# Cross attention and the heads in one block, with the first two tiles of the heads loaded in cross attention's last turn

## The reference

```python
x = x + cross_attention(layernorm(x), ctx, ...)   # 16 heads of 64: softmax(q k^T) v, then @ w_out + b_out, times tanh(gate)
x = x + attention_over_heads(layernorm(x), W_Q, W_K, W_V)   # per token, 16 heads of 32: softmax(Q) (softmax(K)^T V)
x = x + mlp(layernorm(x), w_gate, w_up, w_down)   # silu(x wg) * (x wu), then wd; int weights times 1/127
```

## Time and profile before

| | us |
|---|---|
| three runs | 1935.17, 1937.47, 1942.68 (median 1937.47) |
| the profiled execution | 1935.26 |
| its span, first to last instruction | 1933.5 |

### The profile page before, as it was taken

The page is one execution under the profiler, slowest core; times in us unless marked ns, Lnnn a source line. Parts: engine busy times, 40 slices in busy tenths (PEclk is TensorE's granted clock), DMA queues, the critical chain, the costliest instruction groups (busy, mean ns, idle before and its releaser), DMA issues. The chain is left out here.

```text
span 1933.5 us, 36622 instructions
## 1 busy us (share of the span) xinstructions
PE 1869.3 (97%) x14096; PEld 1611.8 (83%) x14096; DVE 1039.6 (54%) x2015; ACT 667.4 (35%) x1356; POOL 558.1 (29%) x546
## 2 busy tenths in 40 slices
PE   6989999999999999999999999599999999999999
PEld 4868888988988898898889889488888788888887
DVE  6614555455455545545554554478889863333322
ACT  3234444444444444444444444231111231111111
POOL 3015335433533543453354345331112000000000
PEclk9989999999999999999999999799999999999999
DMA  7323313322331332233132224623333041001000
GB/s 242 129 80 93 89 54 109 93 70 76 99 97 54 109 88 75 76 98 98 55 109 86 73 80 131 181 78 99 98 114 111 31 150 42 24 23 43 13 31 22
DMA packets 166629, 165.65 MB, mean 86 GB/s; under 512 B 8688, under 2 KB 123888, under 8 KB 166576
## 3 DMA queue, kind: packets, MB, share of 16 engines
q1 hardware_dynamic: 162144, 156.27, 26.7%
q10 hardware_dynamic: 4432, 8.65, 1.2%
HBM read 131.08 MB, written 33.82 MB: 85 GB/s over the span
## 5 line engine op out<-in xcount | busy, mean ns | idle before, releaser
L497 POOL TENSOR_TENSOR x_prob<-x_prob,x_share 128x256 f32<-128x256 f32 x256 | 157.0, 613 | 621.6 <-DVE x_share L664 614.3
L82 PE MATMUL x_ps<-w_cT_hi,w_space_hi 128*128 128x258 f32 x1024 | 299.2, 292 | 5.8 <-DVE w_space_lo L688 5.8
L83 PE MATMUL x_ps<-w_cT_lo,w_space_hi 128*128 128x258 f32 x1024 | 290.2, 283 | 0.0
L84 PE MATMUL x_ps<-w_cT_hi,w_space_lo 128*128 128x258 f32 x1024 | 288.9, 282 | 0.0
L681 DVE COPY x_mix<-x_ps 128x512 f32<-128x512 f32 x256 | 176.1, 688 | 115.2 <-PE x_ps L84 115.1
L688 DVE TENSOR_TENSOR w_space_lo<-x_ps,w_space_hi 128x512 fp32r<-128x512 f32 x256 | 162.5, 682 | 99.6 <-ACT w_space_hi L789 67.2
L82 PE MATMUL x_ps<-x_pT_hi,x_cn_hi 128*128 128x512 f32 x512 | 208.1, 406 | 1.5 <-DVE x_mix L681 1.5
L778 ACT ACTIVATE x_prob<-x_ps,x_negmax 128x257 f32<-128x257 f32 x256 | 121.9, 476 | 240.1 <-DVE x_negmax L659 240.1
L82 PEld LDWEIGHTS x_ps<-w_cT_hi,w_space_hi 128*128 128x128 f32 x1024 | 193.9, 189 | 12.7 <-DVE w_space_lo L688 8.9
L84 PE MATMUL x_ps<-x_pT_hi,x_cn_lo 128*128 128x512 f32 x512 | 201.3, 393 | 0.0
L83 PE MATMUL x_ps<-x_pT_lo,x_cn_hi 128*128 128x512 f32 x512 | 199.7, 390 | 0.0
(11 more groups left out here) (205 smaller groups left out, 3550.1 us busy)
## 6 DMA issues: line engine op xcount, KB each, us to landing
e_raw_T<-ctx_T SPq DMA_DIRECT2D x64, 514.0 KB, 4.0
e_raw_n<-ctx_nat SPq DMA_DIRECT2D x64, 512.0 KB, 3.6
q<-q_q ACTq DMA_DIRECT2D x16, 512.0 KB, 2.8
e_q<-q SPq DMA_DIRECT2D x16, 512.0 KB, 4.1
o_hi<-x_o_hi SPq DMA_DIRECT2D x32, 256.0 KB, 2.6
o_lo<-x_o_lo SPq DMA_DIRECT2D x32, 256.0 KB, 3.1
a_oT_hi<-o_hi SPq DMA_DIRECT2D x16, 512.0 KB, 4.3
a_oT_lo<-o_lo SPq DMA_DIRECT2D x16, 512.0 KB, 5.6
```

The lines of the kernel that those rows point to most:

```text
L82: pe.matmul(out, lhs[0], rhs[0], start=start, stop=False)
L83: pe.matmul(out, lhs[0], rhs[1], start=False, stop=False)
L84: return pe.matmul(out, lhs[1], rhs[0], start=False, stop=stop)
L497: pool.tensor_tensor(prob[:, i, 0:KT * P], prob[:, i, 0:KT * P], share[:, i:i + 1].to_broadcast([P, KT * P]), ALU.mult)\
```

## The change

Cross attention and heads_and_mlp each return their engine programs, and `build` runs both in a single block: no barrier between them. identity (`ident`) and the PSUM tensor are allocated once for both. The tensors of the heads lie in SBUF from the place where those of cross attention begin (`start`), ordered so that what is filled early lies over what cross attention has finished with; those of cross attention move by the size of `ident`.

Parts of the heads' start move into cross attention's last turn. On SP `first_loads(0)` (tile 0) goes in front of the weight pieces 12 to 15, and `first_loads(1)` (tile 1, then mask, bias and gate) behind them, ahead of the first store. On ACT tanh comes ahead of the second output copy; on DVE the bias product comes behind the second output split; on POOL the bias is added to tiles 0 and 1 ahead of the splits of pieces 16 and 18. DVE's splits of pieces 17 and 19 move behind the scaling of tile 0 (`late_weights`). PE begins with a wait for w_out's splits, does the out-projections of tile 0 (bank Y) and tile 1 (bank DOTS) one after the other, then the transposes of tile 0; it has new waits for the later splits ahead of keys and values. SP's first MLP weight piece waits for all 20 splits, tile 2's load for all stores of cross attention, and MLP piece 22 for the store of tile 14. The diff, without changes of indentation and cut to its core:

```diff
-def cross_attention(nc, hw, ahead, ...):
-    with ExitStack() as ctx:
+def cross_attention(nc, ctx, ps, ident, hw, ahead, ...):
-        ident = s.sb("ident", [P, P])
-        ps = s.psum()
-        block = ctx.enter_context(nc.Block())
-        @block.sync
-        def _(sp):
+    def sync(sp, first_loads):
...
-                    load_w(range(PAIRS + 2, RING + 4))
+                load_w(range(PAIRS + 2, RING))
+                first_loads(0)
+                load_w(range(RING, RING + 4))
+                first_loads(1)
                 store_out(t, 0)
...
-            sp.wait_ge(o_stored.sem, 32 + TURNS * o_stored.per)
...
-                    w_low(pool, range(0, PIECES, 2))
+                w_low(pool, range(0, 16, 2))
+                first_bias()
+                w_low(pool, range(16, PIECES, 2))
...
                 low_out(t, 1)
                 if not more:
-                    w_low(dve, range(15, PIECES, 2))
+                first_bias()
+                w_low(dve, (15,))
...
                     w_high(range(RING, 16))
+                first_tanh()
                 high_out(t, 1)
...
+    def late_weights(dve):
+        w_low(dve, range(17, PIECES, 2))
...
-        area = Area(nc, "a", nc.sbuf_base)
+    area = Area(nc, "a", start)
...
+    def first_loads(sp, part):
+        c, last = cross, cross.last
+        if part == 0:
+            sp.wait_ge(c.mixed.sem, c.mixed.at(last, 3 * c.mixed.per // c.batches))
+            sp.wait_ge(c.turned.sem, c.turned.at(last, c.turned.per))
+            sp.wait_ge(c.last_ready.sem, c.last_ready.at(last, c.batches))
+        sp.wait_ge(c.o_stored.sem, c.o_stored.at(part + 1, 0))
+        load(sp, 0, part)
+        if part == 1:
+            sp.wait_ge(c.mixed.sem, c.mixed.at(last, c.mixed.per))
+            for dst, src in ((mask[:, :], same_token), (gated_bias[:, :], bias.partition_broadcast(P)),
+                             (gate_b[:, :], gate.partition_broadcast(P))):
+                sp.dma_start(dst, src).then_inc(once, 16)
...
                     sp.wait_ge(y_ready.sem, y_ready.at(t, i + 1))
                     sp.wait_ge(x1_done.sem, x1_done.at(t, i + 1))
-                    load(t, i + 2)
+                if tile_of(t, i) == 0:
+                    sp.wait_ge(cross.o_stored.sem, cross.o_stored.at(cross.last + 1, 0))
+                load(sp, t, i + 2)
...
             def load_w(numbers):
                 for n in numbers:
+                if n == 0:
+                    for done in cross.w_lo_done:
+                        sp.wait_ge(done, len(hw.pieces) // 2)
...
-            for dst, src in ((ident[:, :], identity), (mask[:, :], same_token),
-                             (gated_bias[:, :], bias.partition_broadcast(P)), (gate_b[:, :], gate.partition_broadcast(P))):
-                sp.dma_start(dst, src).then_inc(once, 16)
-            load(0, 0)
-            load(0, 1)
             load_w(range(RING))
...
+    def first_rows(pool):
+        pool.wait_ge(bias_done, 1)
+        add_bias(pool, 0, 0)
+        add_bias(pool, 0, 1)
...
             def step(t, i):
+            if tile_of(t, i) == 0:
+                add_out(t, 1, DOTS)
...
-                if there(t, i + 1):
-                    pe.wait_ge(in_loaded[(i + 1) % 2].sem, in_loaded[(i + 1) % 2].at(t, 48 * ((i + 1) // 2 + 1)))
+            if there(t, i + 1) and tile_of(t, i) != 0:
                     if there(t, i - 1):
                         pe.wait_ge(q_shift.sem, q_shift.at(t, i))
+                add_out(t, i + 1, Y)
...
                     pe.wait_ge(o_done.sem, o_done.at(t, i - 1))
+                if tile_of(t, i) == 0:
+                    weights_done(16)
                     project(t, i, 1, K, k_ready)
...
+                if tile_of(t, i) == 0:
+                    weights_done(20)
                     pe.wait_ge(rows_done.sem, rows_done.at(t, i))
                     project(t, i, 2, V, v_ready)
...
+        def weights_done(pieces):
+            for done in cross.w_lo_done:
+                pe.wait_ge(done, pieces // 2)
+
+        def add_out(t, i, bank):
+            pe.wait_ge(in_loaded[i % 2].sem, in_loaded[i % 2].at(t, 48 * (i // 2 + 1)))
+            for j in range(PAIRS):
+                mm = three(pe, ps[:, bank, :], [a[:, j, :] for a in oT[i % 2]], [a[j] for a in wo], j == 0, j == PAIRS - 1)
+            mm.then_inc(y_ready.sem, 1)
...
-            pe.wait_ge(once, 64)
+        weights_done(PAIRS)
             all_steps(pe, step)
...
+    def first_tanh(act):
+        act.wait_ge(once, 48)
+        act.activation(tanh_b[:, :], gate_b[:, :], ACT.Tanh).then_inc(tanh_done, 1)
...
+    def first_bias(dve):
+        dve.wait_ge(once, 48)
+        dve.wait_ge(tanh_done, 1)
+        dve.tensor_scalar(gated_bias[:, :], gated_bias[:, :], tanh_b[:, 0:1], None, ALU.mult).then_inc(bias_done, 1)
...
                     norm_scale(dve, xn, src, moments, rstd, 1).then_inc(normed.sem, 1)
+                if tile_of(t, n) == 0:
+                    cross.late_weights(dve)
...
+        s = Scope(nc, ctx, "s")
+        ident, ps = s.sb("ident", [P, P]), s.psum()
+        start = nc.sbuf_base
...
+        block = ctx.enter_context(nc.Block())
+        @block.sync
+        def _(sp):
+            cross.sync(sp, lambda part: first_loads(sp, part))
+            late.sync(sp)
...
```

More of the change, by code:

```diff
@@ L320, in _, with cross_attention @@
                     mm.then_inc(q_ready.sem, 1)
-def cross_attention(nc, hw, ahead, ctx_nat, ctx_T, last_T, q_dram, v_dram, o_hi, o_lo, identity, heads):
+def cross_attention(nc, ctx, ps, ident, hw, ahead, ctx_nat, ctx_T, last_T, q_dram, v_dram, o_hi, o_lo, identity, heads):
     B, SK, dim = ctx_nat.shape
@@ new lines, in cross_attention @@
+    s = Scope(nc, ctx, "x")
+    wk, w_v, q, raw_n, raw_T = ahead.wk, ahead.w_v, ahead.q, ahead.raw_n, ahead.raw_T
+    fold = hw.fold
+    mix = s.sb("mix", [P, DC, GB, heads * SQ])
+    cn = [s.pair(f"cn{i}", [P, KT, dim]) for i in range(2)]
+    cT = hw.cT
+    prob = s.sb("prob", [P, TILES, SKE])
+    pT = [s.pair(f"pT{i}", [P, KT, heads * SQ]) for i in range(2)]
+    last_p = s.sb("last_p", [P, TILES, GB, SQ])
+    last_v = s.sb("last_v", [P, inner])
+    last_z, last_t = s.sb("last_z", [P, TILES, SQ]), s.sb("last_t", [P, TILES, SQ])
@@ L923, in pair, with heads_and_mlp @@
         return self.sb(name + "_hi", shape, F32R), self.sb(name + "_lo", shape, F32R)
-def heads_and_mlp(nc, ahead, hw, x, bias, gate, o_hi, o_lo, x2, identity, same_token, wg, wu, wd, out, scale):
+def heads_and_mlp(nc, ctx, ps, ident, start, cross, ahead, hw, x, bias, gate, o_hi, o_lo, x2, identity, same_token, wg, wu, wd, out, scale):
     tokens, dim = x.shape
@@ new lines, in heads_and_mlp @@
+    x2o = [area.sb("x2o0", [P, dim])]
+    over = area.at
+    oT = [None, area.pair("oT1", [P, PAIRS, P])]
+    on_oT = [Area(nc, "f1", over), None]
+    on_y = Area(nc, "fy", area.at)
+    x1 = [area.sb(f"x1{i}", [P, dim]) for i in range(4)]
+    xin = [area.sb(f"xin{i}", [P, dim]) for i in range(2)]
+    area.at += 64
+    on_oT[1] = Area(nc, "f0", area.at)
+    oT[0] = area.pair("oT0", [P, PAIRS, P])
+    gated_bias = area.sb("bias", [P, dim])
+    x2o.append(area.sb("x2o1", [P, dim]))
+    mask = area.sb("mask", [P, P])
@@ L1602, in build @@
+    return Programs(sync=sync, gpsimd=gpsimd, tensor=tensor, vector=vector, scalar=scalar), \
+        (first_loads, first_rows, first_tanh, first_bias)
+@dataclass
+class Programs:
+    sync: object
+    gpsimd: object
+    tensor: object
+    vector: object
+    scalar: object
+@dataclass
+class AfterCross:
+    mixed: Count
+    turned: Count
+    last_ready: Count
+    o_stored: Count
+    w_lo_done: list
+    late_weights: object
+    last: int
+    batches: int
 def build(nc, x, ctx_nat, ctx_T, last_T, gamma, beta, wq, wkT, wv, w_out, b_out, gate, aq, ak, av, wg, wu, wd,
```

2028 lines of the change are left out of this document (1005 added, 1023 removed).

## The result

| | before | after | ratio, 95% interval |
|---|---|---|---|
| median of the runs, us | 1937.5 | 1924.6 | 0.993, 0.991 to 0.995 |
| profiled execution, us (span) | 1935.26 (1933.5) | 1922.15 (1920.4) | |
| mean granted clock of TensorE | 0.989 | 0.996 | |

What follows compares the result with a forecast made beforehand. TensorE was taken to bound the kernel, with 24.6 us lost at the seam between cross attention and heads; 2.2 us remain after. 1936.4 - 22.5 = 1913.9 us, own range 1911 to 1917, 8 in 10 range 1909 to 1921.

Steps and rivals of the forecast that it cites:

- The early loads: Seam after cross attention: loads of tiles 0 and 1 go out in the last turn; PE's idle 15.88 us become 0.
- The bias at 1230.2: Seam: the bias product comes at 1230.2, POOL adds it until 1232.7; 1.5 us early, costing nothing.
- the sum: Tile 2's out-projection starts at 1250.0 instead of 1272.47: 22.5 us gone.
- Second out-projection until 1238.9: Seam: two out-projections back to back at full clock hide tile 0's normalisation, 1 to 1.5 us to spare; idle 4.14 us go.
- Keys at 1240.95: Heads' start: new wait for the split of tile 0's transposes, 2.07 us with hand-over, before the keys.
- All splits done at 1238.8: Heads' start: DVE's late weight splits cost 0.68 us each, not 1.76; SP's six MLP weight loads wait for them.
- Tile 2 at 1250.0: Heads' start: tile 2's load lands at 1250.0, behind six weight loads; PE waits 0.55 us more.
- rival E: Cross attention loop: moved tensors lengthen DVE's splits, kernel slower than before, about 1950 us; chance 0.03.
- A: Heads' start: tile 2 lands at 1253 to 1254, PE stands 4 us, clock falls; gain 16 us, 1920; chance 0.15.
- B: Seam: tile 0's normalisation is late behind POOL's bias additions and splits; gain about 19 us, 1917; chance 0.08.
- D: Seam: early loads stuck in SP's queue, PE waits 4.7 us for tile 1; gain 15 us, 1921; chance 0.04.
- rival C: Heads' start: tile 2 lands by 1249.4, better than forecast; gain 23 to 24.6 us, 1912 to 1913; chance 0.08.

Runs made afterwards that it cites:

- e6: The changed kernel with MLP gaps of 128 and 192 bytes, loads of tiles 0 and 1 issued behind the last weights: 1926.2 us, ratio 0.995.
- e5: The changed kernel with MLP gaps of 128 and 192 bytes, tile 0 transposed between the two out-projections as before: 1918.6 us, ratio 0.991.
- e1: The changed kernel with m_xT 128 and h 192 bytes later, at the weights' address modulo 256 again: 1913.9 us, ratio 0.988.
- e2: The kernel before with m_xT 128 and h 64 bytes later, apart from the weights modulo 256 as in the changed kernel: 1944.4 us, ratio 1.004.
- e10: The changed kernel run once more, nothing altered: 1923.0 us, ratio 0.993.
- e3: The changed kernel with only m_xT moved 128 bytes later, h left at 0 modulo 256: 1918.2 us, ratio 0.991.
- e7: The changed kernel with SBUF gaps that put nearly all 512-column matmul operands at equal addresses modulo 256: 1911.2 us, ratio 0.987.

## Why the prediction was wrong

What held, step by step (forecast, then the profile of after):

1. The early loads. Tile 0 issued from 1210.6: 1210.20. Tile 1 after 1217.4: 1217.22. The first store keeps its 1224.67: 1224.50. No wait for either tile. e6 shows that this step is worth some 12 us.
2. The bias at 1230.2: 1229.75 + 0.48. POOL's two additions until 1232.7: 1230.31 + 2.92 = 1233.23, just ahead of y. (The pair took 2.92 us for the 2.54 of the sum, which cost nothing.)
3. Second out-projection until 1238.9: 1238.64; xn at 1237.2 to 1238.1: 1237.04. The margin was 1.6 us, and e5 shows what stands behind it.
4. Keys at 1240.95: 1240.65, the new wait 1.41 us where its first row shows it.
5. All splits done at 1238.8: 1238.23, so a late split cost 0.64, and 0.68 was the right one of the two prices. SP's six loads at 1238.8: 1238.32. Tile 2 at 1250.0: POOL starts on it at 1249.07, and PE waits for nothing, where 0.55 us were forecast.

The rows of SP, POOL and DVE behind these points (timelines of after; SPq rows are times of issuing):

```profile
1210.20 0.38 SPq L1092 DMA_DIRECT2D a_oT_hi<-o_hi  x1
...
1217.22 0.43 SPq L1092 DMA_DIRECT2D a_oT_hi<-o_hi  x1
...
1230.31 2.92 POOL L1159 TENSOR_TENSOR a_xin<-a_xin,a_bias 128x512 f32<-128x512 f32 x2 [3.00 <-DVE a_bias L1443]
...
1236.49 0.55 DVE L141 TENSOR_SCALAR a_xn<-a_x,a_moments,a_rstd 128x512 f32<-128x512 f32 x1 [0.74 <-POOL a_rstd L1170]
1236.95 1.28 DVE L391 TENSOR_TENSOR w_space_lo<-e_wk,w_space_hi 128x512 fp32r<-128x512 f32 x2
...
1238.32 1.78 SPq L1128 DMA_DIRECT2D f_raw<-wg  x4
...
1242.21 3.05 SPq L1094 DMA_DIRECT2D a_xin<-x  x1
...
1249.07 1.29 POOL L1159 TENSOR_TENSOR a_xin<-a_xin,a_bias 128x512 f32<-128x512 f32 x1 [6.03 <-DMA a_xin<-x]
```

What failed is one sentence behind the sum: "Placement in SBUF, the merged block, shared identity and PSUM ... I cost at 0". The MLP got 10.0 us longer in the profile, and the placement accounts for most of it: 768 gate and up matmuls of chunks 1 and 2 x 6.3 ns = 4.8, 384 of chunk 0 x 4 = 1.5, 576 down x 5.4 = 3.1, in all 9.4. Put back, the two tensors give 9.2 us in the MLP of e1's trace, and taken away from before (e2) they cost 9.1 there and 8.8 in the runs. The last 0.9 us between the MLP of before and of e1 has no cause shown. With the placement put right (e1) the kernel takes 21.7 us less than before on its chip, against the 22.5 of the sum. That its 1913.9 us is the forecast's number to the digit is chance: the forecast started from 1936.4, and before takes 1935.6 there.

The sentence that let it through stood in rival E: "No row shows an operation whose length depends on its place". The trace of before did show one. Its MLP chunk 0 (weights at 128, m_xT at 192) ran at 229 ns and the other chunks at 227, with the same shape, engine and helper. By name the group means stood at 393 ns against 389 (groups by line and shape, of before, over the MLP):

```profile
L83 PE MATMUL a_ps<-a_m_xT_lo,f_wg_hi 128*128 128x512 f32 x64 | 25.2, 393 | 0.0
...
L83 PE MATMUL a_ps<-a_m_xT_lo,fhi_wg 128*128 128x512 f32 x64 | 24.9, 389 | 0.0
```

E looked for the effect in the wrong engine (DVE) and the wrong stage (the cross attention, whose pT and cn kept their distance). It priced "slower than before" only, and had no case for a smaller gain by the same mechanism. The mechanism of the seam was right as forecast; the sum failed on this one term. A bound was at hand: by these two means 4 ns x 1728 matmuls = 7 us, which would have carried the range to 1928.

Here the Trainium skill has a rule that would have argued for the zero. "SBUF — State Buffer", Who interferes with whom, gives TensorE two independent read ports, one for the moving operand and one for the weight load, and says that "PE and ACT never wait on anyone". Read so that TensorE's own two reads don't disturb each other either, it has e1 and e2 change nothing. The runs differ: 1924.6 against 1913.9 us and 1935.6 against 1944.4 us for some bytes of gap, so for the pace of a row of matmuls the measurement decides. That it is these two reads which meet isn't shown by any run.

Rivals A, B and D did not occur: no wait for tile 2, for xn or for x shows in after. At the seam this trace looks like rival C, tile 2 a little early and 23.2 us gained, but e10's, of the same kernel, has 21.8: forecast and C can't be told apart. In e10 POOL starts on tile 2 at 1250.62, just ahead of PE's 1250.69, so tile 2 is close to being what sets the time.

## What to carry to other kernels

Where tensors move in SBUF, in a kernel that TensorE bounds, count what the move costs as an edit of its own: list the start addresses modulo 256 of the moving and stationary operand of each kind of matmul, before and after. Compare the distance between matmul starts (or the number of matmuls in a window of fixed length) in a stage that the change doesn't touch; a full busy share at full clock doesn't show a pace 3% slower. Gaps of 128 and 192 bytes gave about 9 us here (e1). Where a stage follows another one, leave out its first six to ten matmuls when you read its pace.

## What the runs showed of the hardware

- In dense rows a 128x512 matmul starts 226.7 ns after the one before where both operands begin at the same address modulo 256 bytes, 229.1 to 230.0 ns where the moving one is 64 above, and 232.4 to 233.4 ns where it is 128 or 192 above (the last three are means of unlike distances, 229 and 238 ns for instance). The windows of the MLP show a granted clock of 1.00 at either pace. Distances finer than 64 bytes weren't tried, and why the distance counts isn't shown.
- A row with equal residues doesn't always start at that pace. In e3, behind down matmuls with unequal residues, the first six gate matmuls are at 228 to 236 ns; in e1, behind ones with equal residues, at 226.7. In e7 the first ten mix matmuls of a run are at 231.5 ns. The second half of the out-projection in e7 has equal residues and follows a half whose residues are unequal in part: its first eight are at 229 to 236 ns, its last four at 226.7. What carries over stays open.
- A pause of TensorE of 1.41 us (after) leaves the granted clock at 1.00. In one of 3.75 us (e5) it falls to 0.50 before PE goes on at 1237.26 and is at 1.00 again from 1241. In one of 8.27 us (e6) it is at 0.50 from 1231, PE goes on at 1236.27, and it is at 1.00 again from 1242.
